# Summing column numbers on TensorE in the two routing sorts of a macaron FFN / Mamba layer, and clearing semaphores in ranges

## What is computed

```python
x = x + 0.5 * ffn(layernorm(x), router_w, w1, w2)
x = x + mamba2(layernorm(x), W_in, conv_w, conv_b, dt_bias, A_log, D, norm_weight, W_out)
x = x + 0.5 * ffn(layernorm(x), router_w, w1, w2)
# ffn: logits = x @ router_w.T ; top 2 of 8 experts, softmax over the two
#      y_e = square(relu(x @ w1[e])) @ w2[e]     (256 -> 512 -> 256)
#      out = weight_1 * y_e1 + weight_2 * y_e2
```

## Time and profile before

| | |
|---|---|
| time of the profiled execution | 1326.81 us |
| its span, first to last instruction | 1325.1 us |
| runs without profile | 1326.93, 1328.05, 1328.78 us |
| PE busy | 1055.2 us (80%) |
| DVE busy | 822.2 us (62%) |
| POOL busy | 686.4 us (52%) |
| ACT busy | 607.5 us (46%) |

### The profile page before, as it was taken

The page is one execution under the profiler, slowest core; times in us unless marked ns, Lnnn a source line. Parts: engine busy times, 40 slices in busy tenths (PEclk is TensorE's granted clock), DMA queues, the critical chain, the costliest instruction groups (busy, mean ns, idle before and its releaser), DMA issues. The chain is left out here.

```text
span 1325.1 us, 21803 instructions
## 1 busy us (share of the span) xinstructions
PE 1055.2 (80%) x6372; PEld 879.8 (66%) x6404; DVE 822.2 (62%) x1609; ACT 607.5 (46%) x1462; POOL 686.4 (52%) x611
## 2 busy tenths in 40 slices
PE   3747999999915788998889898989447999999900
PEld 3735999999914566666667666666336999999800
DVE  6974444444427899898989897875283444444433
ACT  2312555555513565655656555555213555555400
POOL 6945555555421365655564655567344555555300
PEclk9999999999966898888989898989757999999955
DMA  7761222222232111111111100000152222222187
GB/s 238 254 270 45 76 76 78 77 79 77 57 109 72 48 36 41 41 41 40 41 41 40 40 25 17 17 21 24 49 230 60 77 76 79 77 78 77 53 273 238
DMA packets 73243, 112.20 MB, mean 85 GB/s; under 512 B 10664, under 2 KB 60336, under 8 KB 71856
## 3 DMA queue, kind: packets, MB, share of 16 engines
q1 hardware_dynamic: 47888, 58.77, 13.0%
q0 software_dynamic: 13824, 37.77, 8.8%
q10 hardware_dynamic: 11424, 14.30, 3.2%
HBM read 66.76 MB, written 44.04 MB: 84 GB/s over the span
## 5 line engine op out<-in xcount | busy, mean ns | idle before, releaser
L401 POOL DMA_INDIRECT ys_d<-xs,row_of x144 | 142.0, 986 | 194.4 <-DVE xs L765 188.6
L754 DVE TENSOR_TENSOR xl<-pT,xh 128x256 fp32r<-128x256 f32 x144 | 61.1, 424 | 223.3 <-ACT xh L472 223.3
L459 ACT ACTIVATE hs<-pH 128x512 f32<-128x512 f32 x144 | 86.0, 597 | 233.1 <-PE pH L570 233.1
L396 POOL DMA_INDIRECT xs<-xn_d,token_of x144 | 139.8, 971 | 52.1 <-issue 42.3
L759 DVE TENSOR_TENSOR h2l<-hs,h2h 128x512 fp32r<-128x512 f32 x144 | 99.8, 693 | 77.7 <-ACT h2h L467 77.7
L1534 DVE SCALAR_TENSOR_TENSOR acc<-raw,cwh,acc 128x512 f32<-128x512 f32 x104 | 124.8, 1246 | 2.2 <-POOL acc L1061 1.2
L1157 ACT ACTIVATE ex<-bank,dts 128x128 f32<-128x128 f32 x256 | 72.4, 366 | 98.7 <-PE bank L1302 97.0
L590 PE MATMUL pY<-w2h,h2h 128*128 x576 | 102.9, 300 | 0.4 <-DVE h2l L759 0.3
L570 PE MATMUL pH<-w1h,xh 128*128 x288 | 92.7, 404 | 1.8 <-DVE xl L754 1.0
L570 PE MATMUL pH<-w1l,xh 128*128 x288 | 92.4, 403 | 0.0
L590 PE MATMUL pY<-w2h,h2l 128*128 x576 | 92.2, 282 | 0.0
(11 more groups left out here) (244 smaller groups left out, 2650.1 us busy)
## 6 DMA issues: line engine op xcount, KB each, us to landing
m_yg<-ys_d SPq DMA_DIRECT2D x64, 128.0 KB, 2.1
xs<-ys_d SPq DMA_DIRECT2D x16, 512.0 KB, 5.9
wst<-in_L_ffn_w_dram ACTq DMA_DIRECT2D x8, 512.0 KB, 4.4
xs<-in_L_attn_x_dram SPq DMA_DIRECT2D x8, 512.0 KB, 6.5
hs<-in_L_ffn_w_dram ACTq DMA_DIRECT2D x8, 512.0 KB, 4.8
xn_d<-xs SPq DMA_DIRECT2D x8, 512.0 KB, 3.2
lo_d<-w1l SPq DMA_DIRECT2D x1, 4096.0 KB, 11.1
lo_d<-w2l SPq DMA_DIRECT2D x1, 4096.0 KB, 21.3
```

Of the source, the lines that this page charges most:

```text
L396: pool.indirect_dma_start(out=xg[:, t % NX, :], out_offset=None, in_=xn_d, in_offset=bass.IndirectOffsetOnAxis(ap=token_of[:, t:t + 1], ax ...
L401: pool.indirect_dma_start(out=ys_d, out_offset=bass.IndirectOffsetOnAxis(ap=row_of[:, t:t + 1], axis=0), in_=y[:, t % NX, :], in_offset=No ...
L459: act.activation(r[:, u, :], pH[u][:, :], ACT.Relu).then_inc(relu_done.sem, 1)
```

## The change

Two things are changed. First, in both sorts the product of `ohhi` with the column number is no longer made on POOL, and the constant `colnum` goes. The column number is written as the first number of its group of four columns (`SUB` = 4) plus 0 to 3. ACT makes `ohhi_c` as `ohhi` times the first number of the group, in two instructions per piece with a constant scale. What is left, 0 to 3, is summed on PE by its two bits: for columns whose low bit is set, `ohhi` itself is multiplied with `ohlo` into `pT[1]`; for columns whose high bit is set it goes into a third bank, `pH[0]`, and DVE adds this twice at the end. Two waits on `w_lo` stand where ACT and PE had known through POOL's products that the weights are split. Second, `Sems.clear` collects semaphore numbers that follow each other into ranges and clears each range with one instruction.

```diff
+SUB = 4
@@ Sems.clear
-                for s in self.all:
-                    sp.sem_clear(s)
+                nums = sorted(s.num for s in self.all)
+                while nums:
+                    n = 1
+                    while n < len(nums) and nums[n] == nums[0] + n:
+                        n += 1
+                    sp.sem_clear(range(nums[0], nums[0] + n))
+                    nums = nums[n:]
@@ ffn_block, gpsimd
-            pool.iota(colnum[:, :], pattern=[[1, C]], base=1, channel_multiplier=0,
-                      allow_small_or_imprecise_dtypes=True)
...
-            oh_col.open(pool)
-            for piece in range(C // PC):
-                at, u = slice(piece * PC, (piece + 1) * PC), piece % 2
-                pool.wait_ge(oh_hi.sem, oh_hi.done(piece))
-                pool.tensor_tensor(ohhi_c[:, u, :, :], ohhi[:, u, :, :], along(colnum[:, at], NT), ALU.mult).then_inc(oh_col.sem, 1)
@@ ffn_block, scalar
                 act.wait_ge(oh_hi.sem, oh_hi.done(piece))
+                if piece >= 2:
+                    act.wait_ge(oh_used.sem, oh_used.done(piece - 2))
                 act.activation(ohhi_p[:, u, :, :], ohhi[:, u, :, :], ACT.Copy, scale=c["part"][:, 0:1]).then_inc(oh_part.sem, 1)
+                for q in range(PC // SUB):
+                    part = slice(q * SUB, (q + 1) * SUB)
+                    last = act.activation(ohhi_c[:, u, part, :], ohhi[:, u, part, :], ACT.Copy, scale=float(piece * PC + q * SUB + 1))
+                last.then_inc(oh_col.sem, 1)
...
+            if first:
+                act.wait_ge(w_lo.sem, w_lo.done(NW - 1))
             relu(0, 0)
@@ ffn_block, tensor
                 for n in range(PC):
-                    ends = dict(start=(piece == 0 and n == 0), stop=(piece == C // PC - 1 and n == PC - 1))
-                    pe.matmul(pT[0][0:NT, 0:P], ohhi_p[:, piece % 2, n, :], ohlo[:, piece % 2, n, :], **ends)
-                    last = pe.matmul(pT[1][0:NT, 0:P], ohhi_c[:, piece % 2, n, :], ohlo[:, piece % 2, n, :], **ends)
+                    begin, end = piece == 0 and n == 0, piece == C // PC - 1 and n == PC - 1
+                    lo = ohlo[:, piece % 2, n, :]
+                    pe.matmul(pT[0][0:NT, 0:P], ohhi_p[:, piece % 2, n, :], lo, start=begin, stop=end)
+                    if n % SUB % 2:
+                        pe.matmul(pT[1][0:NT, 0:P], ohhi[:, piece % 2, n, :], lo, start=False, stop=False)
+                    if n % SUB >= 2:
+                        pe.matmul(pH[0][0:NT, 0:P], ohhi[:, piece % 2, n, :], lo, start=(piece == 0 and n == 2), stop=end)
+                    last = pe.matmul(pT[1][0:NT, 0:P], ohhi_c[:, piece % 2, n, :], lo, start=begin, stop=end)
                 last.then_inc(oh_used.sem, 1)
...
+            if first:
+                pe.wait_ge(w_lo.sem, w_lo.done(NW - 1))
             pe.wait_ge(experts_known, 1)
@@ ffn_block, vector
-            link(dve.tensor_copy(inv2[0:NT, :], pT[1][0:NT, 0:P]))
+            link(dve.tensor_copy(inv[0:NT, :], pT[1][0:NT, 0:P]))
+            link(dve.scalar_tensor_tensor(inv2[0:NT, :], pH[0][0:NT, 0:P], 2.0, inv[0:NT, :], ALU.mult, ALU.add))
             dve.scalar_tensor_tensor(inv[0:NT, :], inv2[0:NT, :], float(P), pT[0][0:NT, 0:P], ALU.mult, ALU.add).then_inc(inv_ready, 1)
```

More of the change, by code:

```diff
@@ L190, in ffn_block @@
         iota_j = sb("iota_j" + tag, [P, NT, E], F32)
-        colnum = sb("colnum" + tag, [P, C], F32)
         slots = sb("slots" + tag, [P, C], U32)
@@ L415, in _ @@
         def _(act):
-            for s in (xT_copied, logit_copied, oh_part, relu_done, sq_done, g_hi):
+            for s in (xT_copied, logit_copied, oh_part, oh_col, relu_done, sq_done, g_hi):
                 s.open(act)
```

## The result

The kernel after took 1306.21 us (median of 5 runs, 1305.3 to 1312.65) against 1327.99 us for the kernel before (5 runs). The ratio is 0.9849, 95% interval 0.983 to 0.9869, so 21.8 us faster, which is also what the prediction's sum gave. Five more runs on another occasion gave 1306.74 us against 1326.28 us, ratio 0.9846 (0.9821 to 0.9871), 19.5 us faster.

What follows compares the result with a forecast made beforehand. Clears were taken as critical path for 12.8 us, the sorts as bound by a two-piece loop through POOL's product. 12.75 + 0.14 + 2 x (4.76 - 0.32) = 21.8 us gain, forecast 1306.5 us, whole range 1302.5 to 1314.

Steps and rivals of the forecast that it cites:

- (a): SyncE's semaphore clears at the ends of parts: 12.8 us become about 0.05 us, gain 12.75 us.
- the rival that built on it: A range is cleared one semaphore after another: 6.1 us of the 12.8 stay, 1312.3 us; chance 10%.
- (b): POOL in the second part: without the colnum iota, spare starts 0.14 us earlier, gain 0.14 us.
- (c): DVE in the sorts: ohhi takes 0.76 us, DVE's own pace is 1.81 us a piece.
- (d): ACT in the sorts: two new instructions of 0.41 us each, overlapping, so a piece takes 1.37 us.
- (e): PE in the sorts: 24 matmuls a piece, clock rises after some 5 us, spacing then 0.060 us; gain 4.76 us a sort.
- The rival with 0.0875 us: Clock rises in the sorts, but matmuls are spaced at about 0.0875 us: 1310.0 us; chance 17%.
- (f): DVE at each sort's end: one more PSUM instruction costs 0.32 us.
- (g): The waits of PE and ACT on w_lo cost nothing, since POOL splits the weights before its gathers.
- The rival of a clock that outlives the sort: Clock stays up over the gathering, so each FFN's first tiles save up to 2 us: 1302.4 us; chance 7%.
- the clock stays low in the sorts: Rival: PE stays at the low clock in both sorts, total gain 14.75 us, 1313.3 us; chance 18%.
- The slower case: Rival: the sequencer walks a cleared range at over 0.12 us a semaphore, making the kernel slower; chance 2%.

Runs made afterwards that it cites:

- a2: The kernel after, unchanged, run and profiled once more on another chip; 1306.74 us.
- e3: The kernel after with SUB = 1: ACT scales each column by itself, 16 matmuls a piece, no third bank; 1306.9 us, ratio 0.9845.
- e5: The kernel after plus a POOL product on constant data in each piece, which nobody reads or waits for; 1318.66 us against 1306.74.
- e4: The kernel after with SUB = 2: 20 matmuls and four ACT instructions a piece, no third bank; 1303.77 us, ratio 0.9822.
- e1: The kernel before with the range clears alone, its sorts as before; 1314.45 us against 1326.22, ratio 0.9916.

## Why the prediction was right, step by step

(a) Clears: the mechanism held, the size was 12.3 us and not 12.75. A range isn't free of its length: 34 ns for one semaphore, 123 to 128 for 58, 175 for the longest. That is 1.6 ns for each more (94 / 57), far from the 30 ns of my upper bound, and the rival that built on it is out. The sign of being wrong that I had named, a duration that grows with the range, did show, but it is worth 0.4 us in place of 6.1.

(b) The iota: `iota_j` to `spare` was 957.40 to 958.63, now 949.84 to 950.93, 0.14 us less, as said.

(c), (d) DVE and ACT: `ohhi` at 0.76 us as said. ACT takes 86.38 to 87.82 = 1.44 us and not 1.37, since its two instructions are 0.43 us each. The overlap was right. PE waits for ACT before every piece once the clock is up (0.45 us in the first sort, 0.30 to 0.99 in the second), also between the two pieces of a pair, which I had named as a sign of being wrong; it costs nothing beyond the sum, as the loop of two pieces sets the pace.

(e) PE: 0.107 us between starts at the low clock, as said; the rise came after 3.8 and 4.8 us (2.9 and 4.9 in a2), where I had put 5. At the high clock 0.0557 us and not 0.060, so PE's part is 1.28 + 0.22 = 1.50 us. The two errors cancel in the loop: 974.59 to 978.50 is 3.91 us for two pieces against 3.95. The sorts end after 18.85 and about 19.4 us, against 19.48. The rival with 0.0875 us is out. The 81 ns of the Trainium skill ("TensorE: Matmul & The Clock Gate", "Back-to-back issue gap") don't hold here, for weight loads of 72 columns, where the trace has 56 ns, which is the page's own figure for matmuls alone.

The reason that I gave for the clock was only half of it. e3 shows that pieces of 16 matmuls raise it as well. In the kernel before PE's wait for POOL's product left 0.86 us between every two pieces, the first two included. e3 has no product and e5 has the product but nobody who waits for it, and in both the clock rose: as far as these runs show, it was that wait that kept it down. The eight added matmuls go with a clock that stays up afterwards, where e3's fell; that they are the reason is argued and not shown.

The reading of the loop before was also too narrow. I took PE's wait for the product as the bound and DVE's 1.30 us as a part of it. e5 shows that DVE's being held up sets a pace of 2.76 us by itself, with PE waiting for nobody's product. Both bounds stood at the same place, and a change that had only moved the product off PE's path would have gained little in the sorts: e5's are 0.7 us shorter than before, each.

(f) One more DVE instruction, 104.53 to 104.85 = 0.32 us, as said. (g) The waits on `w_lo` cost nothing: in the first profile POOL's last low part ends at 71.8 us, before the sort begins.

The sum in measured terms is 12.3 + 0.14 + (24.67 + 24.68 - 19.42 - 20.12) = 22.3 us, against 21.8 forecast and 21.8 and 19.5 measured. That the forecast and the first measurement agree to a tenth is luck, since the second differs from it by 2.3 us; that the clears came out within 0.5 us and each sort within 0.8 us (4.44 us of gain forecast, 5.25 and 4.56 measured in a2) is not. What the sum doesn't hold is the tiles: in the first FFN they are 0.6 to 1 us longer in after's two profiles, though not in e3 and e4. In the first profile PE is dense from 113.11 and its matmuls shorten only at 119.2 us, 6 us later, against 4.0 us before (117.71 to 121.71):

```profile
113.11 1.22 PE L581 MATMUL pH<-w1h,xh 128*128 x2 [1.06 <-DVE xl L768]
...
118.82 0.79 PE L590 MATMUL pR<-ident,hs 128*128 128x128 f32 x4
119.36 0.71 PE L581 MATMUL pH<-w1h,xh 128*128 x2
119.91 0.62 PE L581 MATMUL pH<-w1l,xh 128*128 x2
```

The rival of a clock that outlives the sort came closer than I had thought. In the second sort the last of its matmuls ends at 984.49, and the clock stays up with PE almost idle and falls at about 989.6, just before the first tile's matmul at 990.04:

```profile
986.00:988.00 2.00, 0.00 (x0) 0.00 (x0) 1.83 (x8) 0.00 (x0) 0.87 (x1) 1.00 0.00 0
988.00:990.00 2.00, 0.00 (x0) 0.00 (x0) 0.90 (x2) 0.00 (x0) 1.39 (x3) 0.90 0.20 66
990.00:992.00 2.00, 1.34 (x4) 0.57 (x4) 0.42 (x1) 0.38 (x1) 1.65 (x2) 0.50 0.44 131
```

So the tiles gained nothing from it, and the rival is out. That the clock stays low in the sorts is out as well, in every profile. The slower case needed 0.12 us for each semaphore.

## What to carry to other kernels

Look at the ends of blocks for time that no busy share counts: 202 single clears stood for 12.8 us, and four ranges for 0.5. Where the instructions of two engines hold each other up, as those of DVE and POOL do here, price a moved product by what it does to the other engine's instructions and not only by who waits for it: the same product cost 8 us of the sorts without a single reader. And when PE works in many short pieces, look for the place where they first follow each other without a gap, and at the clock behind it. Redundant matmuls need not cost time: the two sorts together took 40.7 us with 16 matmuls a piece, 38.1 with 20 and 39.5 with 24, though over the whole program the medians of 16 and 24 are the same.

## What the runs showed of the hardware that I had not expected

A range clear costs 34 ns for one semaphore and 123 to 128 ns for 58. The clock, once up, stayed up over 10 us with PE busy only half of the time in e5 (the 24 matmuls of a piece start 0.056 us apart to the end of the sort), and fell in e3 at 99.2 us after a stretch with a similar share (3.38 of the 6.2 us before); what tells the two apart is open:

```profile
95.00:105.00 10.00, 5.05 (x82) 4.70 (x83) 10.00 (x8) 5.35 (x12) 7.32 (x4) 1.00 0.01 2
```

mamba_block, unchanged in all kernels, takes either 570 to 571 or 574.4 to 574.8 us. Its PE clock is 0.87 on average in the short ones but for e1's 0.86, and 0.86 in the long ones, and what sends an execution the one way or the other is not settled. It is the largest part of the 6.2 us between the two profiled runs of after, next to the tiles, and it has to be read before a gain of a few microseconds is believed.
